# In each step of two attention stages on TensorE, the weighted sum is put in front of the scores

## What is computed

```python
def _ln(x, g, b): ...            # (x - mean) * rsqrt(var + EPS) * g + b
def _attn(x, ctx, Wq, Wk, Wv, Wo, bo):
    q, k, v = x @ Wq, ctx @ Wk, ctx @ Wv          # 16 heads of 64 columns each
    sim = jnp.einsum('bihd,bjhd->bhij', q, k) * scale
    attn = jax.nn.softmax(sim, axis=-1)
    out = jnp.einsum('bhij,bjhd->bihd', attn, v).reshape(b, n, INNER)
    return out @ Wo + bo
h = _ln(x, g1, be1)
x = _attn(h, h, Wq1, Wk1, Wv1, Wo1, bo1) + x
h = _ln(x, g2, be2)
x = _attn(h, context, Wq2, Wk2, Wv2, Wo2, bo2) + x
h = _ln(x, g3, be3)
y = h @ Wp + bp
a, gate = (y[..., :FF_HID], y[..., FF_HID:])
x = a * jax.nn.gelu(gate, approximate=False) @ W2 + b2 + x
```

## Time and profile before

| | us |
|---|---|
| median of 3 runs | 3203.68 (3201.36 to 3205.22) |
| the profiled execution | 3205.43 |
| its span, first to last instruction | 3203.6 |
| PE busy in the span | 3112.9 (97%) |
| DVE busy | 2426.6 (76%) |
| ACT busy | 1885.0 (59%) |
| POOL busy | 1365.8 (43%) |

### The profile page before, as it was taken

How to read it: one execution, slowest core, us unless ns; L and a number is a source line. 1 busy time by engine, 2 the same in 40 slices (tenths; PEclk the granted TensorE clock), 3 DMA queues, 4 the chain that set the end, 5 groups by cost and what they waited for, 6 DMA issues and landing times. The chain is left out here.

```text
span 3203.6 us, 81927 instructions
## 1 busy us (share of the span) xinstructions
PE 3112.9 (97%) x25600; PEld 2605.1 (81%) x25600; DVE 2426.6 (76%) x4811; ACT 1885.0 (59%) x5999; POOL 1365.8 (43%) x1295
## 2 busy tenths in 40 slices
PE   7999999999999999699999999999999969999999
PEld 6888888888888888578888888888888858888888
DVE  7777777777777777588888888888888855565655
ACT  6666666666666666466666666666666643232232
POOL 4444444444444444355555555555555520000100
PEclk9999999999999999799999999999999989999999
DMA  8888888888888887588888888888888860000100
GB/s 245 229 229 229 229 229 229 229 229 229 229 229 229 229 229 221 166 236 241 239 240 241 240 240 242 238 241 240 241 243 240 239 170 22 31 26 30 35 26 20
DMA packets 464425, 625.02 MB, mean 195 GB/s; under 512 B 57728, under 2 KB 397056, under 8 KB 464128
## 3 DMA queue, kind: packets, MB, share of 16 engines
q1 hardware_dynamic: 460256, 624.09, 67.8%
q10 hardware_dynamic: 4128, 0.41, 0.1%
HBM read 330.71 MB, written 293.60 MB: 195 GB/s over the span
## 5 line engine op out<-in xcount | busy, mean ns | idle before, releaser
L381 POOL TENSOR_TENSOR self_probs<-self_probs,self_row_inv 128x512 f32<-128x512 f32 x512 | 535.2, 1045 | 628.1 <-DVE self_row_inv L577 627.2
L381 POOL TENSOR_TENSOR cross_probs<-cross_probs,cross_row_inv 128x512 f32<-128x512 f32 x512 | 535.2, 1045 | 591.0 <-DVE cross_row_inv L577 591.0
L414 ACT ACTIVATE cross_probs<-cross_ps_s,cross_neg_max 128x256 f32<-128x256 f32 x1024 | 473.8, 472 | 66.9 <-DVE cross_neg_max L552 56.9
L414 ACT ACTIVATE self_probs<-self_ps_s,self_neg_max 128x256 f32<-128x256 f32 x1024 | 473.6, 472 | 55.0 <-DVE self_neg_max L552 54.6
L552 DVE TENSOR_REDUCE cross_neg_max<-cross_ps_s 128x2 f32<-128x512 f32 x512 | 325.1, 675 | 0.9 <-PE cross_ps_s L735 0.9
L552 DVE TENSOR_REDUCE self_neg_max<-self_ps_s 128x2 f32<-128x512 f32 x512 | 325.0, 675 | 0.9 <-PE self_ps_s L735 0.8
L571 DVE STREAM_TRANSPOSE cross_blocks<-cross_probs 128x1024 f32<-128x1024 f32 x256 | 316.1, 1235 | 0.0
L571 DVE STREAM_TRANSPOSE self_blocks<-self_probs 128x1024 f32<-128x1024 f32 x256 | 316.0, 1234 | 0.0
L561 DVE TENSOR_TENSOR self_qk_lo<-self_ps_qk,self_qk_hi 128x512 fp32r<-128x512 f32 x256 | 177.1, 692 | 172.6 <-ACT self_qk_hi L475 172.6
L466 ACT ACTIVATE self_o_hi<-self_ps_o 128x256 fp32r<-128x256 f32 x256 | 98.2, 384 | 341.7 <-PE self_ps_o L753 341.6
L466 ACT ACTIVATE cross_o_hi<-cross_ps_o 128x256 fp32r<-128x256 f32 x256 | 98.3, 384 | 327.3 <-PE cross_ps_o L753 327.3
(11 more groups left out here) (166 smaller groups left out, 9817.5 us busy)
## 6 DMA issues: line engine op xcount, KB each, us to landing
self_turns<-self_blocks SPq DMA_DIRECT2D x1024, 128.0 KB, 2.5
self_probs_t<-self_turns SPq DMA_DIRECT2D x256, 512.0 KB, 4.4
cross_turns<-cross_blocks SPq DMA_DIRECT2D x1024, 128.0 KB, 2.6
cross_probs_t<-cross_turns SPq DMA_DIRECT2D x256, 512.0 KB, 4.5
self_xt<-in_x SPq DMA_DIRECT2D x32, 256.0 KB, 3.8
self_xres<-in_x SPq DMA_DIRECT2D x32, 256.0 KB, 4.0
after_self_attention<-yout SPq DMA_DIRECT2D x32, 256.0 KB, 2.6
cross_xt<-after_self_attention SPq DMA_DIRECT2D x32, 256.0 KB, 3.6
```

The source lines that it names most:

```text
L381: pool.tensor_tensor(probs[:, slot % 2, h], probs[:, slot % 2, h], scale, ALU.mult).then_inc(probs_ready, 1)
L414: last = act.activation(probs[:, slot % 2, h, t], scores[:, slot % 2, h, t], ACT.Exp, bias=neg_max[:, slot % 2, i:i + 1], accum_out=row_su ...
```

## The change

In PE's `step`, the block of the weighted sum (W) is moved in front of the block of the scores (S). Both blocks, their waits and their increments are the same as before; no other engine's program changes. A step on PE is then QK, V, OUT, transposes, W, S, where it was QK, V, OUT, transposes, S, W.

```diff
--- before.py
+++ after.py
@@ -720,23 +720,6 @@
                         transpose_context(b + 1)
                     if p == TURN_H:
                         transpose_h(b + 1)
-                if alive(part, p, SCORES):
-                    s = g - SCORES
-                    slot = (p - SCORES) % 2
-                    pe.wait_ge(qk_ready, s + 1)
-                    if counts(c := 2 * (s - 1)):
-                        pe.wait_ge(exps_done, c)
-
-                    passes = ((qk_hi, qk_hi), (qk_lo, qk_hi), (qk_hi, qk_lo))
-                    for i, (q, k) in enumerate(passes):
-                        for t in range(TT):
-                            for h in range(2):
-                                rows = HEAD_ROWS[h]
-                                last = nc.tensor.matmul(scores[:, slot, h, t], q[rows, slot, t * P:(t + 1) * P],
-                                                        k[rows, slot, SEQ:2 * SEQ], start=i == 0 and t == 0,
-                                                        stop=i == len(passes) - 1 and t == TT - 1,
-                                                        skip_group_check=True)
-                    last.then_inc(scores_done, 1)
                 if alive(part, p, WEIGHTED):
                     s = g - WEIGHTED
                     q = (p - WEIGHTED) % PAIRS
@@ -754,6 +737,23 @@
                                 ps_o[DHEAD * h:DHEAD * (h + 1), 0:SEQ],
                                 v[:, k, c:c + DHEAD], turned_t[:, h, k], start=k == 0, stop=k == TT - 1)
                     last.then_inc(pv_done, 1)
+                if alive(part, p, SCORES):
+                    s = g - SCORES
+                    slot = (p - SCORES) % 2
+                    pe.wait_ge(qk_ready, s + 1)
+                    if counts(c := 2 * (s - 1)):
+                        pe.wait_ge(exps_done, c)
+
+                    passes = ((qk_hi, qk_hi), (qk_lo, qk_hi), (qk_hi, qk_lo))
+                    for i, (q, k) in enumerate(passes):
+                        for t in range(TT):
+                            for h in range(2):
+                                rows = HEAD_ROWS[h]
+                                last = nc.tensor.matmul(scores[:, slot, h, t], q[rows, slot, t * P:(t + 1) * P],
+                                                        k[rows, slot, SEQ:2 * SEQ], start=i == 0 and t == 0,
+                                                        stop=i == len(passes) - 1 and t == TT - 1,
+                                                        skip_group_check=True)
+                    last.then_inc(scores_done, 1)
 
             pe.wait_ge(ident_made, 2)
             if cross:
```

## The result

| | before | after |
|---|---|---|
| median | 3204.45 us (3201.36 to 3205.53, 4 runs) | 3280.55 us (3275.22 to 3286.28, 4 runs) |
| span of the profiled execution | 3203.6 | 3273.4 |
| 28 self sequences, each | 40.04 | 40.72 |
| 28 cross sequences, each | 39.27 | 40.78 |

What follows compares the result with a forecast made beforehand. PE was taken to bound both attention stages. Self 31 x 0.60 = 18.6, cross 31 x (0.85+0.48) = 41.2, drains 1.5, switches 0: +61 us on 3203.68, so 3265 us; range 3215 to 3300 (0.64 on the forecast).

Steps and rivals of the forecast that it cites:

- The switches: PE's changes between blocks: W-S assumed to cost 0.09 us like the others, so no change; bounds -45 to +35 us.
- o_lo behind the maxima: DVE's queue makes PE's OUT wait in steps 3 and 5: 0.36 us self, 0.48 cross, for each such step.
- steps 3 and 4 together: Self stage: step 3 grows 0.36 us, step 4 gives back 0.12, so +0.24 a sequence.
- step 5: OUT's wait for o_lo, no V to cover it: +0.36 us a self sequence, 0.48 a cross one.
- The load: Cross stage: the earlier W waits 0.99 us a sequence for its load, +0.85 over today's average 0.14.
- Cross steps 3 and 4 together: Forecast unchanged, since DVE's chain still sets step 4's OUT at 7.66 us after step 3's QK.
- hence 0.11+1.62 = 1.73 after QK, against 1.71 today: ACT's qk_hi start in the new order, taken as nearly unmoved, so step 0's turn stays.
- the two drains: Where each stage empties, one step is longer, maxima standing before o_lo: 0.76 us a stage, 1.5 together.
- The signs: What the changed kernel's trace should show: named PE waits, W-S 1.01, S-QK 0.91, maxima 0.1 after QK, sequences of 40.6 us.
- PE's busy time: Expected to stay as before in the changed kernel's trace.
- the 12.7 us of the earlier trace: W's total wait for its load before the change, 30 waits; forecast to rise to about 35 us in cross.

Runs made afterwards that it cites:

- split_sp_ct: `split_sp` with DVE copying the context before normalizing x in step 3 of the cross stage: 3181.84 us, ratio 0.9921 to the kernel before.
- split: Changed kernel with DVE's o_lo put between the two maxima of the step before: 3230.21 us, ratio 1.0075 to the kernel before.
- load_first: Changed kernel with SP issuing the next sequence's loads behind step 1's load of the turned probabilities, not in step 0: 3255.59 us, ratio 1.0155.
- split_sp: Changed kernel with o_lo between the maxima and SP's next loads, store and residual load between `load_turn` and `store_turn`: 3199.05 us, ratio 0.9977.
- olo_first: Changed kernel with DVE's o_lo put in front of both maxima of the step before: 3268.84 us, ratio 1.0198 to the kernel before.
- both: Changed kernel with the changes of `olo_first` and `load_first` together: 3238.91 us, ratio 1.0104 to the kernel before.
- before_sp: Kernel before, old order on PE and DVE, with the SP places of `split_sp`: 3202.51 us, ratio 0.9985 to the kernel before.
- before_sp_ct: `before_sp` with DVE copying the context before normalizing x in step 3 of the cross stage: 3193.11 us, ratio 0.9952 to the kernel before.

## Why the prediction was right

The time fell into the range, 16 us above the number (3280.55 against 3265), and by its own steps, each against the rows of after (steps by their QK starts, means over 30 sequences):

- *The switches.* W to S was taken at 1.01, S to QK at 0.91: 679.82, 680.83, 681.74 give just these. Nothing of the loss lies here, and `split_sp_ct` with PE busy throughout says so again. The Trainium skill, in "TensorEngine Tiling (Array Packing)", section "Key Properties", states a drain at a change of mode, without a length. The rows show no more of it here than at the change from W to QK before: the same 1.01, and S starts 0.07 us before W's recorded end, which is modelled. What a drain costs inside this 1.01 no run here separates.
- *o_lo behind the maxima.* OUT at 1.77 was forecast, 1.79 measured. Measured, with the forecast in brackets, self: steps 3 and 4 together +0.27 (0.24), step 5 +0.38 (0.36). Cross: step 5 +0.50 (0.48). `split` took this away, with the small wait of step 4 that was there before, and gave 50 us.
- *The load.* 0.99 us of waiting a cross sequence in all was read off two rows; steps 1 and 2 of after are 1.07 longer than their passes, and 0.91 longer than before (0.85). `load_first` and `split_sp` confirm it. That a part falls into step 1 was said; it is nearly half.
- *Where it was off.* Cross steps 3 and 4 together were forecast unchanged and grew by 0.16, 5 us in all. The term that was off is "hence 0.11+1.62 = 1.73 after QK, against 1.71 today": 1.71 is the self stage's (it became 1.75). In cross QK has eleven passes and ends sooner, and qk_hi started sooner too, 1.59 after QK in step 3; behind the maxima it starts at 1.75 there as well, 0.16 later. ACT's qk_hi in a cross step 0, before (QK at 2041.85), then after (QK at 2045.64):

```profile
2043.54 0.60 ACT L475 ACTIVATE cross_qk_hi<-cross_ps_qk 128x512 fp32r<-128x512 f32 x1
```

```profile
2047.47 0.60 ACT L475 ACTIVATE cross_qk_hi<-cross_ps_qk 128x512 fp32r<-128x512 f32 x1
```

1.69 became 1.83 in this step, and the turn follows it, 3.16 after QK instead of 3.02; that is why the load's part was short too. In step 3 all that follows qk_hi moves by its 0.16, and the maxima that were to stay at 6.00 start 6.16 after QK (2061.42):

```profile
2065.61 1.44 DVE L518 TENSOR_SCALAR cross_xnorm<-cross_xt,cross_meanvar,cross_rstd 128x256 f32<-128x256 f32 x2
2066.98 0.68 DVE L524 COPY cross_c_t<-cross_ps_misc 128x512 f32<-128x512 f32 x1
2067.58 1.27 DVE L552 TENSOR_REDUCE cross_neg_max<-cross_ps_s 128x2 f32<-128x512 f32 x2
```

A cross sequence grew by 1.54 instead of 1.33 and a self one by 0.68 instead of 0.60 (steps 1 and 2 have 0.03 of it, for which I have no reason), 9 us in all: 61 us become the 70 of the profiled execution. The other 6 of the 76 lie between that execution and the median of the changed kernel's four runs, which spread over 11 us. I have no experiment on that.
- *Luck.* 1.5 us for the two drains came out, but not as reasoned. From the last QK to the last OUT the self drain went from 33.1 to 29.6 us and the cross drain from 27.7 to 32.7, where +0.76 was forecast for each. The granted clock went with it: 0.74 and 0.94 in the two drains of before, 0.88 and 0.74 in those of after.
- *The signs.* The intervals of the switches, the maxima at 0.11 with DVE idle before them, and sequences of 40.72 and 40.78 (40.6 forecast for each) came as named. PE's busy time did not stay: it rose by 24 us, since a matmul's modelled end covers a part of each wait. And the view behind the 12.7 us of the earlier trace rows gives 51.7 in after instead of about 35; it counts PE's weight loads beside the matmuls. From start to start the waits are 1.07 a cross sequence, 33 us.

What the prediction had no eye for came out only in the experiments: how near the next waits were. Each wait that was removed let another one through (the late turn, the low part of the context, the context copy). Six of the ten expectations missed their number, four of them for this (`olo_first`, `both`, `split`, `split_sp`).

## What to carry to other kernels

When an engine's block is moved within a loop, its own engine need not be where the price is; here it was not. Ask behind what its consumer stands in the consumer's queue (here o_lo behind two maxima), and how long before its use each input lands (here a load that had 0.04 us to spare). Both can be read off the timeline before the change, by steps and for each kind of step, since only the short steps (no V) and the steps with late loads paid. A new order must bring the consumers' orders along: alone it cost 76 us, with o_lo, the loads and the store on SP and one copy in new places the kernel was 26 us faster than before, 15 of which the old order gets as well.

## What the runs showed of the hardware

DVE's normalization (L518, from SBUF to SBUF) is two equal instructions. Beside POOL's scaling of the probabilities one of them takes longer. The groups of `before_sp` and of `before_sp_ct`, where the copy out of PSUM stands first and the normalization meets less of POOL's operation:

```profile
L518 DVE TENSOR_SCALAR cross_xnorm<-cross_xt,cross_meanvar,cross_rstd 128x256 f32<-128x256 f32 x64 | 45.3, 750 | 0.9 <-POOL cross_rstd L344 0.9
```

```profile
L518 DVE TENSOR_SCALAR cross_xnorm<-cross_xt,cross_meanvar,cross_rstd 128x256 f32<-128x256 f32 x64 | 34.4, 578 | 0.9 <-POOL cross_rstd L344 0.9
```

750 ns on average against 578. In `before_sp` the single durations go from 0.39 to 1.13 us. In time, `before_sp`:

```profile
2012.21 1.44 DVE L518 TENSOR_SCALAR cross_xnorm<-cross_xt,cross_meanvar,cross_rstd 128x256 f32<-128x256 f32 x2
...
2012.37 1.13 POOL L381 TENSOR_TENSOR cross_probs<-cross_probs,cross_row_inv 128x512 f32<-128x512 f32 x1 [1.22 <-DVE cross_row_inv L577]
...
2014.17 1.27 DVE L552 TENSOR_REDUCE cross_neg_max<-cross_ps_s 128x2 f32<-128x512 f32 x2
```

and `before_sp_ct`:

```profile
2009.17 0.67 DVE L524 COPY cross_c_t<-cross_ps_misc 128x512 f32<-128x512 f32 x1
2009.75 1.09 DVE L518 TENSOR_SCALAR cross_xnorm<-cross_xt,cross_meanvar,cross_rstd 128x256 f32<-128x256 f32 x2
2010.76 1.28 DVE L552 TENSOR_REDUCE cross_neg_max<-cross_ps_s 128x2 f32<-128x512 f32 x2
...
2009.33 1.04 POOL L381 TENSOR_TENSOR cross_probs<-cross_probs,cross_row_inv 128x512 f32<-128x512 f32 x1 [1.23 <-DVE cross_row_inv L577]
```

Step 3's QK is at 2008.18 and at 2005.14. The copy beside POOL takes 0.67 as ever, and the pair of normalizations 1.09 instead of 1.44: 0.35 of the 0.37 us by which the maxima of step 3 come sooner. The long normalization waits for POOL's end: in these two traces all 124 that last over 0.6 us, in both stages, end 0.15 us after POOL's operation does, whether they last 1.13 us or, started later beside it as in `before_sp_ct`, 0.76. POOL's own operation, started while the first normalization ran, takes 1.13 instead of 1.04 in `before_sp`. The Trainium skill, in "Advanced Engine Details and Errata", section "VectorE Performance Modes", says that the second SBUF port of VectorE is shared with GpSimd, so that VectorE's two-port instructions and GpSimd's block each other; the rows agree with that. That these instructions run in a two-port mode was not tested. So the port as the reason is the page's; the wait for POOL's end and its cost are the rows'.
